# A two-layer expert kernel: the products of layer one and layer two alternate by nine instead of by 27

## The chip, the cores and the metric

The kernel runs on one core of a Trainium2 chip. Its time is the device time in microseconds of one execution. Five engines work side by side and meet only at semaphores: TensorE (PE in the rows, PEld for its weight loads), VectorE (DVE), ScalarE (ACT), GpSimd (POOL) and SyncE (SP), which issues the DMAs.

## The reference

The input x is 32 images of 384 channels and 28 x 28 = 784 pixels. What is computed:

```
xn     = group_norm(x, 32 groups)                         # per image
scores = softmax(xn @ gate_w + gate_b)                    # 4 experts, per pixel
coef   = softmax of the two best scores, given to the experts that were
         picked anywhere as first (weight 0) or second (weight 1)
hdn[e] = relu(w1[e] @ xn + b1[e])                         # 384 -> 384
y[e]   = w2[e] @ hdn[e] + b2[e]                           # 384 -> 384
out    = x + sum over e of coef[e] * y[e]
```

All four experts run on all pixels.

## The kernel before

**Tiles, units, chunks.** The 32 x 784 pixels are cut into 49 tiles of 512 pixels, across image borders. A unit u is one expert of one tile (u = 4t + e, 196 units). A chunk q = 3u + k is one of its three blocks of 128 hidden channels (588 chunks, twelve a tile). Every float32 factor is split into a high and a low part, and a product of two such factors is three matmuls (low x high, high x low, high x high) of 128 x 128 weights with 512 columns. So a chunk of layer one (`mm1`, L432 to L434, into one of the four PSUM banks of `z_ps`) is nine matmuls, and a chunk of layer two (`mm2`, L451 to L453, into the three banks of `y_ps`) is nine as well. `y_ps` adds up over all four experts of a tile.

**One chunk's way.** `mm1` finishes chunk q in `z_ps` and signals `z_ready`. On DVE `scale` (L479) adds the bias and multiplies by the expert's coefficient row, into one of three `hid` buffers; ACT's `split_h_hi` (L486) makes the rounded relu; DVE's `split_h_lo` (L490) the remainder. Then `mm2` of that chunk may run (it waits for `hlo_ready`). In DVE's program, iteration q holds `scale(q + 1)` and then `split_h_lo(q)`, and after these whatever else is due. `mm1` of chunk q waits until `scale` has read chunk q - 4, since there are four banks. After the last `mm2` of a tile (`unit_done`) DVE's `add_product` (L508, three instructions, one for each bank of `y_ps`) adds the product to `res`, which SP then stores; the first `mm2` chunk of the next tile waits, bank by bank, for these three (`out_ready`, L450). `add_product` of tile t - 1 stands in DVE's program at the head of iteration q = 12t + 2.

**What else DVE does.** Every image has to be prepared in good time for its first tile. The pieces hang on chunk numbers (`preparing`): in the tile three before the image's first one, at its chunks 10 and 11, the statistics (L245, and L251 to L262 behind them); in the next tile at chunk 1 the columns of the normalisation (L270 to L273) and half of the normalisation (L278), at chunk 2 the other half, at chunks 8 to 11 the gate (L317 to L358), the last of which makes `wrow`. For images 2 to 31 the first half of the normalisation is thus the last thing ahead of `add_product`. SP writes `wrow` to DRAM (`rows_out`, L524), and reads it back spread over the partitions, for a whole tile (`rows_in`, L531): these are the coefficient rows that `scale` needs from the tile's first chunk on. Image 1 is prepared by hand in tile 0, at q = 2 to 9.

**TensorE's order.** It is written out by hand. The warm-up, the gate product of image 0, and layer one of units 0, 1 and two thirds of unit 2 come first. Then for each unit u: gate products that are due (`gate_product`, L300, 24 short matmuls into `g_ps`), all of `mm1` of unit u + 1 (27 matmuls), the gate product of image 1 if u is 2, and all of `mm2` of unit u (27 matmuls).

Of the kernel before, what the change touches and what calls it, by code (L numbers as in the profile page):

```python
# [9 lines left out]
NK = HID // P  # L10
# [10 lines left out]
UNITS = TILES * E  # L21
# [25 lines left out]
def parts_to(t):  # L47

    return sum(PIECES[:t + 1])
# [7 lines left out]
def first_tile(n):  # L57
    return n * PIX // T
# [6 lines left out]
def conv_moe(nc, x, gate_w, gate_b, w1, b1, w2, b2, out):  # L65
# [7 lines left out]
    with ctx:  # L73
# [6 lines left out]
        def sem(name):  # L80
            return ctx.enter_context(nc.semaphore(name))
# [105 lines left out]
        unit_done = sem("unit_done")  # L187
# [108 lines left out]
        def gate_product(pe, s, n, q):  # L296
            pe.wait_ge(s.xn_ready, HALVES * (n + 1))
            for j in range(NJ):
                for g in range(4):
                    ins = nc.tensor.matmul(g_ps[32 * g:32 * (g + 1), 0:QUART], gw_pad[:, j],  # L300
                                           x_raw[:, q, j, g * QUART:(g + 1) * QUART],
                                           start=(j == 0), stop=(j == NJ - 1), tile_position=(0, 32 * g))
            ins.then_inc(s.gate_ready, 1)
# [70 lines left out]
        def sum_counts(pe, s):  # L374
            pe.wait_ge(s.cnt_ready, 1)
            nc.tensor.matmul(g_ps[:, 0:2 * E], ones[:, :], cnt[:, :, :].rearrange("p r e -> p (r e)"),
                             start=True, stop=True).then_inc(s.cnt_summed, 1)
# [12 lines left out]
        def mm1_early(pe, u, chunks, terms, counts=False):  # L390


            for i, term in enumerate(terms):
                if term == "hl":
                    pe.wait_ge(main.xlo_ready, 1)
                if term == "lh":
                    pe.wait_ge(w1lo_ready, u + 1)
                if term == "hh":
                    pe.wait_ge(main.xhi_ready, 1)
                    pe.wait_ge(whi_ready[0], u + 1)  # L400
                for k in chunks:
                    q = NK * u + k
                    if i == 0 and q >= ZB:
                        pe.wait_ge(early_done, q - ZB + 1)
                    ks = slice(k * P, (k + 1) * P)
                    for j in range(NJ):
                        w = (w1_hi, w1_lo)[term[0] == "l"][:, u, j, ks]
                        x = (x_hi, x_lo)[term[1] == "l"][:, 0, j]
                        ins = nc.tensor.matmul(z_ps[:, q % ZB], w, x, start=(i == 0 and j == 0),
                                               stop=(i == 2 and j == NJ - 1))  # L410
                    if counts and i == 0 and k == 0:
                        sum_counts(pe, main)
                    if i == 2:
                        ins.then_inc(z_ready, 1)

        def mm1(pe, u, chunks=range(NK)):
            t, e = divmod(u, E)
            if t == 0:
                pe.wait_ge(w1lo_ready, 1 + e)
            if e == 0:  # L420
                pe.wait_ge(main.xlo_ready, parts_to(t))
            for k in chunks:
                q = NK * u + k
                if q < ZB + EARLY:
                    pe.wait_ge(early_done, q - ZB + 1)
                else:
                    pe.wait_ge(scaled, q - ZB + 1)
                z = z_ps[:, q % ZB]
                ks = slice(k * P, (k + 1) * P)
                for j in range(NJ):  # L430
                    hi, lo = x_hi[:, t % 2, j], x_lo[:, t % 2, j]
                    nc.tensor.matmul(z, w1_hi[:, e, j, ks], lo, start=(j == 0), stop=False)  # L432
                    nc.tensor.matmul(z, w1_lo[:, e, j, ks], hi, start=False, stop=False)  # L433
                    ins = nc.tensor.matmul(z, w1_hi[:, e, j, ks], hi, start=False, stop=(j == NJ - 1))  # L434
                ins.then_inc(z_ready, 1)

        def mm2(pe, u):
            t, e = divmod(u, E)
            tail = u == UNITS - 1
            if t == 0:  # L440
                pe.wait_ge(w2lo_ready, 1 + e)
            for k in range(NK):
                slot = (NK * u + k) % RING
                pe.wait_ge(hlo_ready, NK * u + k + 1)
                for m in range(NJ):
                    y = y_ps[:, m]
                    ms = slice(m * P, (m + 1) * P)
                    first, last = e == 0 and k == 0, e == E - 1 and k == NK - 1
                    if first and t:
                        pe.wait_ge(out_ready, t * NJ - NJ + m + 1)  # L450
                    nc.tensor.matmul(y, w2_hi[:, e, k, ms], h_lo[:, slot], start=first, stop=False)  # L451
                    nc.tensor.matmul(y, w2_lo[:, e, k, ms], h_hi[:, slot], start=False, stop=False)  # L452
                    ins = nc.tensor.matmul(y, w2_hi[:, e, k, ms], h_hi[:, slot], start=False, stop=last)  # L453
                    if tail and k == NK - 1:
                        ins.then_inc(tail_product, 1)
            if not tail:
                ins.then_inc(unit_done, 1)

        def relu_early(act, q):
            act.wait_ge(z_ready, q + 1)  # L460
# [363 lines left out]
        @block.tensor  # L824
        def _(pe):
            pe.wait_ge(gw_ready, 1)
            pe.wait_ge(main.var_ready, 1)
            for _ in range(WARM):
                nc.tensor.matmul(g_ps[:, 0:P], ones[:, :], ones[:, :], start=True, stop=True)
            gate_product(pe, main, 0, 0)  # L830
            mm1_early(pe, 0, range(NK), ("hh", "lh", "hl"))
            mm1_early(pe, 1, range(NK), ("hh", "hl", "lh"), counts=True)
            mm1_early(pe, 2, range(2), ("hh", "hl", "lh"))
            pe.wait_ge(flag_ready, 1)
            flag = pe.value_load(missing[0:1, 0:1], min_val=0, max_val=1)
            with pe.If(flag > 0):
                with pe.Fori(1, B) as b:
                    gate_product(pe, scan, b - 1, 2)
                sum_counts(pe, scan)

            for u in range(UNITS):
                for n in range(2, B):
                    if NK * u == TILE_CHUNKS * first_tile(n) - LEAD + 8:
                        gate_product(pe, main, n, n % SLOTS)
                if 0 < u < UNITS - 1:
                    mm1(pe, u + 1, chunks=range(2 if u == 1 else 0, NK))
                if u == 2:
                    gate_product(pe, main, 1, 1)
                mm2(pe, u)


# [24 lines left out]
```

## Time and profile before

| | |
|---|---|
| median of 3 runs | 2469.34 us (2468.12 to 2470.34) |
| the profiled execution | 2469.91 us |
| its span, first to last instruction | 2468.1 us |
| mean granted TensorE clock | 0.999 |
| TensorE busy | 2449.9 us, 99% of the span |
| VectorE busy | 1413.7 us, 57% |
| ScalarE busy | 465.6 us, 19% |
| data moved | 189.58 MB, mean 77 GB/s |

The span leaves out 1.8 us of the profiled execution that lie before the first or after the last instruction. A matmul's row is longer than the distance to the next one, since matmuls overlap; the pace is the distance between starts. Idle time of an engine is listed with what ended it.

### The profile page before, as it was taken

How to read it: one execution, taken by the hardware profiler on the slowest of the kernel's cores; microseconds unless marked ns; L12 is line 12 of the kernel's file. 1: busy time of each engine (PE TensorE's matmuls, PEld its weight loads, DVE VectorE, ACT ScalarE, POOL GpSimd, SP SyncE). 2: the span in 40 equal slices, each digit the busy share in tenths (PEclk: the TensorE clock that was granted, in tenths of full speed). 3: DMA queues.
4: the chain of work that ended last, by engine and by line, in shares of the span. 5: the costliest groups of instructions: out<-in, count | busy, mean ns of one | idle time of the engine just before them, and what ended most of it. 6: DMA issues, size and time to landing. Idle time of an engine off the chain costs nothing.

```text
span 2468.1 us, 27782 instructions
## 1 busy us (share of the span) xinstructions
PE 2449.9 (99%) x11372; PEld 2011.4 (81%) x11372; DVE 1413.7 (57%) x2952; ACT 465.6 (19%) x777; POOL 53.3 (2%) x36
## 2 busy tenths in 40 slices
PE   7999999999999999999999999999999999999999
PEld 6788888888888888888888888888888888888887
DVE  7765556556564556545564565556556564556443
ACT  3121111111111121111111121112111111121111
POOL 0000000000000000000000000000000000000000
PEclk9999999999999999999999999999999999999999
DMA  5223122221222213111321123121221222113110
GB/s 185 90 80 104 49 90 69 94 67 49 90 92 71 67 52 123 58 69 49 113 70 69 67 77 107 49 90 69 94 67 49 90 94 68 67 51 108 54 47 26
DMA packets 127520, 189.58 MB, mean 77 GB/s; under 512 B 16032, under 2 KB 80800, under 8 KB 127392
## 3 DMA queue, kind: packets, MB, share of 16 engines
q1 hardware_dynamic: 127392, 187.80, 22.5%
q8 instruction: 89, 1.46, 0.2%
q14 instruction: 39, 0.32, 0.0%
HBM read 146.03 MB, written 41.75 MB: 76 GB/s over the span
## 4 chain that ended last, share of the span: by engine, by line
PE 98%; DVE 1%; DMA 1%; issue 0%; ACT 0%; POOL 0%; SPq 0%; DVEq 0%; POOLq 0%
PE z_ps L432 16%; PE y_ps L451 16%; PE y_ps L452 16%; PE y_ps L453 16%; PE z_ps L434 16%; PE z_ps L433 16%; PE g_ps L300 1%; DMA rows<-rows_dram 0%; DMA rows_dram<-wrow 0%; DMA x_raw<-in_x 0%; DVE w_lo L386 0%; DVE h_lo L490 0%; DVE x_raw L278 0%; ACT h_hi L486 0%; POOL rstd L267 0%
## 5 line engine op out<-in xcount | busy, mean ns | idle before, releaser
L479 DVE SCALAR_TENSOR_TENSOR hid<-z_ps,b_sb,rows 128x512 f32<-128x512 f32 x584 | 436.7, 748 | 896.2 <-PE z_ps L434 892.9
L451 PE MATMUL y_ps<-h_lo,w_hi 128*128 128x512 f32 x1764 | 687.6, 390 | 4.2 <-DVE h_lo L490 4.2
L452 PE MATMUL y_ps<-h_hi,w_lo 128*128 128x512 f32 x1764 | 687.0, 389 | 0.0
L453 PE MATMUL y_ps<-h_hi,w_hi 128*128 128x512 f32 x1764 | 686.9, 389 | 0.0
L432 PE MATMUL z_ps<-x_lo,w_hi 128*128 128x512 f32 x1740 | 680.8, 391 | 0.0
L434 PE MATMUL z_ps<-x_hi,w_hi 128*128 128x512 f32 x1740 | 677.5, 389 | 0.0
L433 PE MATMUL z_ps<-x_hi,w_lo 128*128 128x512 f32 x1740 | 677.0, 389 | 0.0
L486 ACT ACTIVATE h_hi<-hid 128x512 fp32r<-128x512 f32 x588 | 368.6, 631 | 1554.4 <-DVE hid L479 1549.2
L490 DVE SCALAR_TENSOR_TENSOR h_lo<-hid,h_hi 128x512 fp32r<-128x512 f32 x588 | 401.0, 682 | 5.1 <-ACT h_hi L486 4.5
L451 PEld LDWEIGHTS y_ps<-h_lo,w_hi 128*128 128x128 f32 x1764 | 331.6, 188 | 74.4 <-issue 3.1
L432 PEld LDWEIGHTS z_ps<-x_lo,w_hi 128*128 128x128 f32 x1740 | 326.6, 188 | 76.0 <-issue 9.3
L453 PEld LDWEIGHTS y_ps<-h_hi,w_hi 128*128 128x128 f32 x1764 | 331.6, 188 | 68.9
L452 PEld LDWEIGHTS y_ps<-h_hi,w_lo 128*128 128x128 f32 x1764 | 331.6, 188 | 68.5
L434 PEld LDWEIGHTS z_ps<-x_hi,w_hi 128*128 128x128 f32 x1740 | 326.7, 188 | 68.5
L433 PEld LDWEIGHTS z_ps<-x_hi,w_lo 128*128 128x128 f32 x1740 | 326.8, 188 | 67.0
L508 DVE SCALAR_TENSOR_TENSOR res<-y_ps,bias,res 128x512 f32<-128x512 f32 x147 | 101.1, 743 | 111.5 <-PE y_ps L453 111.5
L497 DVE SCALAR_TENSOR_TENSOR res<-rows,bias_gap,res 128x512 f32<-128x512 f32 x147 | 101.5, 746 | 0.0
L267 POOL TENSOR_TENSOR rstd<-gvar_eps,minus_half 128x8 f32<-128x8 f32 x32 | 53.1, 1659 | 2216.7 <-DVE gvar_eps L262 2216.7
L245 DVE BATCH_NORM_STATS2 st<-x_raw 128x6 f32<-128x392 f32 x186 | 92.3, 552 | 0.0
L292 DVE TENSOR_TENSOR x_lo<-x_raw,x_hi 128x1536 fp32r<-128x1536 f32 (+31 forms) x80 | 90.3, 1129 | 0.0
L286 ACT CAST x_hi<-x_raw 128x1536 fp32r<-128x1536 f32 (+31 forms) x80 | 77.1, 964 | 8.8 <-DVE x_raw L278 8.8
L278 DVE TENSOR_SCALAR x_raw<-x_raw,norm 128x1176 f32<-128x1176 f32 (+1 forms) x64 | 69.8, 1093 | 1.2
(88 smaller groups left out, 374.3 us busy)
## 6 DMA issues: line engine op xcount, KB each, us to landing
rows<-rows_dram SPq DMA_DIRECT2D x48, 1280.0 KB, 6.1
x_raw<-in_x SPq DMA_DIRECT2D x62, 588.0 KB, 6.0
res<-in_x SPq DMA_DIRECT2D x18, 768.0 KB, 5.5
out<-res SPq DMA_DIRECT2D x17, 768.0 KB, 4.3
rows_dram<-wrow SPq DMA_DIRECT2D x32, 98.0 KB
w_in<-in_w SPq DMA_DIRECT2D x3, 576.0 KB, 9.9
res<-in_x SPq DMA_DIRECT2D x2, 744.0 KB, 4.9
out<-res SPq DMA_DIRECT2D x2, 744.0 KB, 4.1
```

The lines of the kernel that those rows point to most:

```text
L245: ins = nc.vector.bn_stats(st6[:, HALVES * j + h], x_raw[:, q, j, half(h)])
L432: nc.tensor.matmul(z, w1_hi[:, e, j, ks], lo, start=(j == 0), stop=False)
L433: nc.tensor.matmul(z, w1_lo[:, e, j, ks], hi, start=False, stop=False)
L434: ins = nc.tensor.matmul(z, w1_hi[:, e, j, ks], hi, start=False, stop=(j == NJ - 1))
L451: nc.tensor.matmul(y, w2_hi[:, e, k, ms], h_lo[:, slot], start=first, stop=False)
L452: nc.tensor.matmul(y, w2_lo[:, e, k, ms], h_hi[:, slot], start=False, stop=False)
L453: ins = nc.tensor.matmul(y, w2_hi[:, e, k, ms], h_hi[:, slot], start=False, stop=last)
L479: nc.vector.scalar_tensor_tensor(hid[:, q % HIDS], z_ps[:, q % ZB], b1_sb[:, e, k:k + 1], coef, ALU.add, ALU.mult).then_inc(scaled, 1)
L486: nc.scalar.activation(h_hi[:, q % RING], hid[:, q % HIDS], ACT.Relu).then_inc(hhi_ready, 1)
L490: nc.vector.scalar_tensor_tensor(h_lo[:, q % RING], hid[:, q % HIDS], 0.0, h_hi[:, q % RING].bitcast(f32), ALU.max, ALU.subtract).then_inc ...
L497: lk.inc(nc.vector.scalar_tensor_tensor(xs, rows[:, t % 2, E], bias_gap[:, m:m + 1], xs, ALU.mult, ALU.add))
L508: nc.vector.scalar_tensor_tensor(xs, y_ps[:, m], bias01[:, 1, m:m + 1], xs, ALU.add, ALU.add).then_inc(out_ready, 1)
```

## The change

`mm2` takes the chunks that it is to do, as `mm1` did already, and TensorE's loop goes through the three chunks of a unit, `mm1` of one chunk of unit u + 1 and then `mm2` of the same chunk number of unit u. The matmuls are the same ones. The gate product of image 1, in unit 2, now comes ahead of `mm1` of unit 3, since it stands before the loop over chunks. `unit_done` is still signalled by the unit's last matmul. The other engines' programs are as before.

```
-        def mm2(pe, u):
+        def mm2(pe, u, chunks):
...
-            for k in range(NK):
+            for k in chunks:
...
-            if not tail:
-                ins.then_inc(unit_done, 1)
+                if k == NK - 1 and not tail:
+                    ins.then_inc(unit_done, 1)
...
-                if 0 < u < UNITS - 1:
-                    mm1(pe, u + 1, chunks=range(2 if u == 1 else 0, NK))
                 if u == 2:
                     gate_product(pe, main, 1, 1)
-                mm2(pe, u)
+                for c in range(NK):
+                    if 1 < u < UNITS - 1 or (u == 1 and c == 2):
+                        mm1(pe, u + 1, chunks=[c])
+                    mm2(pe, u, [c])
```

## Rows read from the trace of the kernel before

**Rows 1.** The page: busy time by engine.

```profile
PE 2449.9 (99%) x11372; PEld 2011.4 (81%) x11372; DVE 1413.7 (57%) x2952; ACT 465.6 (19%) x777; POOL 53.3 (2%) x36
```

**Rows 2.** TensorE's waits: us in total, times, longest.

```profile
PE g_ps L829 <- DVE gw_pad L576: 10.4, 1, 10.4
PE y_ps L451 <- DVE h_lo L490: 4.2, 2, 2.1
```

**Rows 3.** Windows: length, PE, PEld, DVE, ACT, POOL busy, clock, DMA, GB/s.

```profile
35.00:38.30 3.30, 3.30 (x8) 2.65 (x9) 3.30 (x7) 1.26 (x2) 0.00 (x0) 0.51 1.04 376
...
77.00:85.00 8.00, 8.00 (x35) 6.61 (x36) 7.61 (x22) 2.53 (x3) 1.64 (x1) 1.00 0.14 51
...
1000.00:2440.00 1440.00, 1440.00 (x6677) 1183.12 (x6677) 807.69 (x1649) 266.29 (x448) 27.83 (x17) 1.00 0.21 72
```

**Rows 4.** Timeline of TensorE: start, length, instruction.

```profile
64.51 0.39 PE L432 MATMUL z_ps<-x_lo,w_hi 128*128 128x512 f32 x1
...
70.40 0.39 PE L434 MATMUL z_ps<-x_hi,w_hi 128*128 128x512 f32 x1
70.63 0.39 PE L451 MATMUL y_ps<-h_lo,w_hi 128*128 128x512 f32 x1
```

**Rows 5.** Timeline of all engines, towards the end.

```profile
2450.06 0.39 PE L434 MATMUL z_ps<-x_hi,w_hi 128*128 128x512 f32 x1
...
2450.55 0.75 DVE L479 SCALAR_TENSOR_TENSOR hid<-z_ps,b_sb,rows 128x512 f32<-128x512 f32 x1 [0.69 <-PE z_ps L434]
...
2452.59 0.75 DVE L479 SCALAR_TENSOR_TENSOR hid<-z_ps,b_sb,rows 128x512 f32<-128x512 f32 x1 [0.69 <-PE z_ps L434]
...
2453.26 1.47 DVE L490 SCALAR_TENSOR_TENSOR h_lo<-hid,h_hi 128x512 fp32r<-128x512 f32 x2
```

**Rows 6.** Timeline of DVE, from chunk 11 of tile 1.

```profile
119.84 0.75 DVE L479 SCALAR_TENSOR_TENSOR hid<-z_ps,b_sb,rows 128x512 f32<-128x512 f32 x1 [4.15 <-PE z_ps L434]
...
127.43 0.74 DVE L479 SCALAR_TENSOR_TENSOR hid<-z_ps,b_sb,rows 128x512 f32<-128x512 f32 x1
...
130.27 2.05 DVE L508 SCALAR_TENSOR_TENSOR res<-y_ps,bias,res 128x512 f32<-128x512 f32 x3
```

**Rows 7.** Timeline of all engines, first matmul of tile 1's layer two.

```profile
84.54 2.05 DVE L508 SCALAR_TENSOR_TENSOR res<-y_ps,bias,res 128x512 f32<-128x512 f32 x3
...
85.08 0.39 PE L434 MATMUL z_ps<-x_hi,w_hi 128*128 128x512 f32 x1
85.39 0.19 PEld L451 LDWEIGHTS y_ps<-h_lo,w_hi 128*128 128x128 f32 x1 [0.34 <-issue]
...
85.98 0.19 PEld L451 LDWEIGHTS y_ps<-h_lo,w_hi 128*128 128x128 f32 x1
```

**Rows 8.** Timeline of DVE, 50 to 76 us.

```profile
50.07 2.09 DVE L278 TENSOR_SCALAR x_raw<-x_raw,norm 128x1176 f32<-128x1176 f32 x2
...
53.55 0.68 DVE L490 SCALAR_TENSOR_TENSOR h_lo<-hid,h_hi 128x512 fp32r<-128x512 f32 x1
58.73 0.41 DVE L317 STREAM_TRANSPOSE lg_pix<-lg_rows 128x224 f32<-128x224 f32 x1 [4.50 <-ACT lg_rows L307]
...
59.72 0.74 DVE L479 SCALAR_TENSOR_TENSOR hid<-z_ps,b_sb,rows 128x512 f32<-128x512 f32 x1
...
62.83 0.75 DVE L479 SCALAR_TENSOR_TENSOR hid<-z_ps,b_sb,rows 128x512 f32<-128x512 f32 x1
...
75.57 0.75 DVE L479 SCALAR_TENSOR_TENSOR hid<-z_ps,b_sb,rows 128x512 f32<-128x512 f32 x1 [3.26 <-DMA rows<-rows_dram]
```

**Rows 9.** Timeline of TensorE in units 2 and 3.

```profile
50.90 0.39 PE L432 MATMUL z_ps<-x_lo,w_hi 128*128 128x512 f32 x1
...
57.11 1.20 PE L300 MATMUL g_ps<-x_raw,gw_pad 128*32 128x196 f32 x24
58.24 0.50 PE L451 MATMUL y_ps<-h_lo,w_hi 128*128 128x512 f32 x1
58.58 0.39 PE L452 MATMUL y_ps<-h_hi,w_lo 128*128 128x512 f32 x1
```

## The prediction, made before the change was run

> **What bounds the kernel now.** I read the page first: TensorE is busy for 2449.9 of 2468.1 us, no other engine for more than 57% [rows 1]. Then the waits of TensorE: 10.4 us before its first matmul and 4.2 us, twice 2.1, for `h_lo` in the first 77 us; beyond these no wait of more than a few tenths is listed [rows 2]. The windows say the same of the long middle: 1440.00 of 1440.00 us busy, at full clock [rows 3]. So the time is the number of matmuls times their pace, plus a start. For the pace I went to TensorE's timeline: 26 distances lie between 64.51 and 70.40, so one is 0.2265 us, and the change from `mm1` to `mm2` at 70.63 is one more such step, 0.23 [rows 4]. Nine matmuls are 2.04 us, eighteen 4.08.
>
> The change removes no matmul and adds none. It can only act by (a) the pace, (b) waits in the steady tiles, (c) the start, (d) the end.
>
> **(a) The pace.** More changes between the layers, six a unit for two, cost nothing where such a change is one plain step [rows 4]. `mm1` in pieces repeats its wait for `x_lo`: two more waits in each of 48 tiles. These have long been met. The waits for `scaled` and `hlo_ready` stood ahead of every chunk before too, with no gap at them. I take nothing. If each of the 96 cost 0.03 us it would be 2.9 us; I have no row for it, and the plain steps across chunks that have such a wait speak for zero.
>
> **(b) The steady tiles.** Three things may come late. I count from S, the start of the matmul that follows layer one's last matmul of chunk 12t + 2. A product's last matmul starts 0.23 before S, and DVE's `scale` starts 0.49 after that start (2450.06, 2450.55 [rows 5]), at S + 0.26.
>
> `h_lo`. `split_h_lo(q)` follows `scale(q + 1)` on DVE, so it needs layer one of chunk q + 1. In the new order 36 matmuls, 8.2 us, lie between that and `mm2` of chunk q (before: 36 for the third chunk of a unit, 63 for the others). DVE needs 0.49 and some 1.4 of this. Its longest iteration, chunk 11 of a tile in which one image ends its gate and another its statistics, with the short iteration after it, takes 119.84 to 127.43, 7.59 us [rows 6]; two chunks give it 8.16. So DVE falls behind by 3.5 us at most and has caught up before chunk 2. The cover holds, with 8.2 - 1.9 - 3.5 = 2.8 us left. Freeing of `z_ps`: 63 matmuls, 54 at least before; more cover. ACT may wait for a gate product ahead of one `split_h_hi`, but its `split_h_lo` waits on DVE for a product which TensorE makes after that gate product, so nothing is later. SP's per-tile loads and stores stand in the same order, at the same pace, with a tile's time (49 us) of cover.
>
> `y_ps`, the tight one. After a tile's last `mm2` there were 27 matmuls of `mm1`, 6.1 us, in which `add_product` could empty `y_ps`; now there are nine, 2.04 us. In 18 tiles DVE only waits for `unit_done`: the add starts at S + 2.04 + 0.26 = S + 2.30. For the images 2 to 31 the columns and half the normalisation stand ahead of it: from the `scale` of chunk 2 to `add_product` 127.43 to 130.27, 2.84 us [rows 6], so it starts at S + 3.10. The first of three adds takes 0.74, and the weight load that waited for it came 0.11 later (84.54 + 0.74 = 85.28, load 85.39 [rows 7]): S + 3.95. It is due one step ahead of the matmul at S + 4.08, at S + 3.85. So it is 0.10 late in 30 tiles, and 0.70 early in the others. What does a late load cost? In tile 1 it was due at 85.08 and came at 85.39, 0.31 late; the next bank's first load came at 85.98 in place of 85.08 + 3 x 0.2265 = 85.76: 0.22 was lost [rows 7]. So some 0.09 are free, and 0.10 late costs about 0.01. The second and third bank follow at 0.66 us on DVE against 0.68 on TensorE, not later. For errors of a few hundredths in each row I take 0.03 a tile, over 29 tiles (tile 1 is counted below): +0.9 us. Bounds: nothing, and 0.25 each (0.34 late) = 7.3 us.
>
> **(c) The start.** Here a chain over DVE and two DMAs decides: gate product of image 1, DVE's gate, `wrow` to DRAM and back, `scale(12)` at 75.57 after a wait for these rows [rows 8], then DVE without a break to `add_product` at 84.54, for which TensorE was 0.22 late at `mm2` of unit 4 [rows 7]. Moved ahead, the gate product waits for image 1's normalisation, which ends at 50.07 + 2.09 = 52.16 [rows 8]. TensorE is there at 50.90 plus the 0.3 that such a product's first load takes [rows 9], so it stands for 1.0 us. The product then runs at 52.2 for 57.11; DVE takes it up when it is free, at 54.15 for 58.73. But `scale(9)` now needs a later product: 52.2 + 1.13 + 0.34 + 7 x 0.2265 + 0.49 = 55.8, for 59.72; and `scale(10)` one 4.08 later, 59.9 for 62.83 [rows 8, 9]. The chain is thus some 3.1 us earlier, not 4.6: rows at 72.4, `split_h_lo(11)` done by 73.8. `mm2` of chunk 11 is due at about 75.8, so the 2.1 us wait goes. `add_product` starts at 81.4. TensorE is at that place at 79.8 already and waits until 82.3, a new wait of 2.4 us. From there to the end of unit 4 it has 45 matmuls left (`mm2` 12, `mm1` 16, `mm2` 13, `mm1` 17, `mm2` 14) where it had 27. So: -3.1 + 18 x 0.2265 = **+1.0 us**. Bounds: if the chain comes no earlier, +4.1; if it is early enough not to be waited for, 1.0 - 2.3 - 0.2 = -1.5.
>
> **(d) The end.** Layer one's last chunk ends nine matmuls before unit 194 does; `scale` to the end of the last `h_lo` takes 2452.59 to 2454.73, 2.1 us [rows 5], and that `h_lo` is due 27 matmuls, 6.1 us, after layer one's end. Nothing.
>
> **Sum.** +1.0 + 0.9 = +1.9 us. The profiled execution took 2469.91, its span 2468.1 and 1.8 around it; it lies 0.6 over the median of 2469.34, within the runs' spread. I add to the median: **2471.2 us**. A measurement of this kernel can tell about 0.2%, 4.9 us, from no change.
>
> **Rivals.** (1) The emptying of `y_ps` is the new bound: slower. All hangs on 0.10 us worked out of 3.95. If the add comes 0.22 later still, since `z_ready` or `unit_done` take longer or DVE is held by something, each of 29 tiles costs 0.22: 6.4 + 1.0, 2476.7. It decides from (4.9 - 1.0) / 29 = 0.13 us a tile. Against it: the rows used are of the same instructions in the same order. (2) The chain at the start is earlier than I have it, and the new wait doesn't arise: 2469.34 - 1.5 = 2467.8, still no change. (3) The new wait of 2.4 us lowers the clock. Of the two waits of 2.1 us [rows 2], the first, up to 35 us, was followed by a granted clock of 0.51 until 38.3, the 1.2 GHz level; after the second, up to 77 us, it stayed 1.00, 2.4 GHz [rows 3]. Eight matmuls took 3.30 us there, 0.41 each for 0.2265: a drop would cost about 1.5 us: 2472.7. (4) The pace itself depends on the order of products, and 0.2265 is not what a matmul must take: at 512 columns and 2.4 GHz the columns alone are 0.2133. If alternating took off half of the 0.013 over it, 10,500 matmuls would give 69 us, 2400. Against it: `z_ps`, nine in a row into one bank, and `y_ps`, three, run at one pace [rows 4]. The Trainium skill (TensorE: Matmul & The Clock Gate, on 56 ns against 53.3) has 215.7 ns for back-to-back matmuls of 512 columns at full clock. The rows here show 226.5 in both layers, so the measurement decides; by the page's pace, reached through the new order, the time would be near 2355 us, an estimate.
>
> **How the numbers follow.** Forecast, near +1.9: 0.62. Rival 1: 0.18, slower by over 0.2%. Rival 2: 0.12 and rival 3: 0.05, both within 0.2%. Rival 4: 0.03, faster. So faster 0.03, within 0.2% 0.79, slower 0.18. The range goes from rival 2, less 0.6 for the spread, 2467.2, to the start's +1.0 with the upper bound of (b), 7.3, a little under 2477.7: 2477.5.
>
> **What would show it.** Right: TensorE 99% busy, the pace still 0.2265; one wait of about 1 us before L300 near 51 us; none before the L451 of chunk 11; one of some 2.4 us before the L451 near 80 us, ended by L508; in 30 tiles the first L451 load at most 0.1 late and `add_product` without idle time ahead of it there. Wrong: L451 waiting for L508 by 0.2 us or more at 30 places (rival 1), waits of L451 for L490 in steady tiles (the cover miscounted), waits of L432 for L479, another distance between matmuls (rival 4), or a granted clock under 1 after 82 us (rival 3).

## The result, and the profile after

The changed kernel takes 2474.70 us (median of 11 runs, 2471.49 to 2476.44), the kernel before 2469.91 in the same comparison (11 runs, 2468.12 to 2471.12). The ratio is 1.0018, with a 95% interval of 1.0011 to 1.0026: some 4.5 us more (4.8 between the two medians). The loss is clear of the noise, and a little under the 0.2% that were taken as the bound of no change. 2471.2 was forecast, 1.9 us more, with a range of 2467.2 to 2477.5. The profiled execution took 2475.36 us, its span 2473.6.

The page of the changed kernel, busy time by engine (answers to [rows 1]):

```profile
PE 2453.0 (99%) x11372; PEld 2010.1 (81%) x11372; DVE 1425.5 (58%) x2952; ACT 471.2 (19%) x777; POOL 53.3 (2%) x36
```

TensorE is as full as before, with the same 11372 matmuls. Its waits in the changed kernel (answers to [rows 2]: us in total, times, longest):

```profile
PE g_ps L829 <- DVE gw_pad L576: 10.4, 1, 10.4
...
PE g_ps L300 <- DVE x_raw L278: 2.7, 1, 2.7
PE y_ps L451 <- DVE res L508: 2.1, 1, 2.1
PE y_ps L451 <- DVE h_lo L490: 1.8, 1, 1.8
```

The second wait for `h_lo` is gone, and the two that were forecast stand there: for image 1's normalisation ahead of its gate product, and for `add_product`. None is listed in a steady tile. So where did the time go? I split the run by two rows that both orders have, the last matmul of tile 1 and that of tile 46. Timeline of TensorE, kernel before:

```profile
129.51 0.39 PE L453 MATMUL y_ps<-h_hi,w_hi 128*128 128x512 f32 x1
...
2372.54 0.39 PE L453 MATMUL y_ps<-h_hi,w_hi 128*128 128x512 f32 x1
```

and changed kernel:

```profile
133.64 0.39 PE L453 MATMUL y_ps<-h_hi,w_hi 128*128 128x512 f32 x1
...
2378.00 0.39 PE L453 MATMUL y_ps<-h_hi,w_hi 128*128 128x512 f32 x1
```

Tiles 2 to 46 took 2243.03 us before and 2244.36 after: +1.3. Tile 1's end comes 4.1 later. The first matmul of layer two, kernel before and changed kernel:

```profile
34.95 0.77 PE L451 MATMUL y_ps<-h_lo,w_hi 128*128 128x512 f32 x1 [2.10 <-DVE h_lo L490]
```

```profile
34.96 0.47 PE L451 MATMUL y_ps<-h_lo,w_hi 128*128 128x512 f32 x1 [1.79 <-DVE h_lo L490]
```

So the start, from there to tile 1's end, went from 94.56 to 98.68. The end adds nothing: the spans differ by 2473.6 - 2468.1 = 5.5 = 4.1 + 1.3, within the rounding.

The start of the changed kernel, timeline of two engines (answers to [rows 8, 9] and the first row of [rows 7]):

```profile
52.22 1.26 PE L300 MATMUL g_ps<-x_raw,gw_pad 128*32 128x196 f32 x24 [2.71 <-DVE x_raw L278]
53.41 0.80 PE L432 MATMUL z_ps<-x_lo,w_hi 128*128 128x512 f32 x1
54.01 0.63 PE L433 MATMUL z_ps<-x_hi,w_lo 128*128 128x512 f32 x1
54.43 0.63 PE L434 MATMUL z_ps<-x_hi,w_hi 128*128 128x512 f32 x1
...
57.35 0.75 DVE L479 SCALAR_TENSOR_TENSOR hid<-z_ps,b_sb,rows 128x512 f32<-128x512 f32 x1 [2.14 <-PE z_ps L434]
...
74.00 0.75 DVE L479 SCALAR_TENSOR_TENSOR hid<-z_ps,b_sb,rows 128x512 f32<-128x512 f32 x1 [3.31 <-DMA rows<-rows_dram]
...
82.96 2.05 DVE L508 SCALAR_TENSOR_TENSOR res<-y_ps,bias,res 128x512 f32<-128x512 f32 x3
83.84 0.66 PE L451 MATMUL y_ps<-h_lo,w_hi 128*128 128x512 f32 x1 [2.12 <-DVE res L508]
84.30 0.63 PE L452 MATMUL y_ps<-h_hi,w_lo 128*128 128x512 f32 x1
84.73 0.63 PE L453 MATMUL y_ps<-h_hi,w_hi 128*128 128x512 f32 x1
```

The reader is to see two things. The gate product begins at 52.22, as forecast; but the matmuls behind it start 0.42 apart (54.01, 54.43), not 0.23, and so `scale(9)` comes at 57.35 where 55.8 was worked out, the rows at 74.00 for 72.4, `add_product` at 82.96 for 81.4. And behind the second wait the matmuls are slow once more. The windows of the changed kernel say why (answers to [rows 3]: length, PE, PEld, DVE, ACT, POOL busy, clock, DMA, GB/s):

```profile
35.00:38.30 3.30, 3.30 (x15) 2.73 (x16) 3.30 (x7) 1.27 (x2) 0.00 (x0) 1.00 1.04 375
53.40:57.00 3.60, 3.60 (x13) 2.87 (x10) 1.71 (x6) 1.07 (x3) 0.00 (x0) 0.55 0.00 0
57.00:81.70 24.70, 24.70 (x110) 20.11 (x108) 19.01 (x60) 4.70 (x8) 1.64 (x1) 1.00 0.35 111
83.80:87.70 3.90, 3.86 (x10) 3.10 (x11) 3.90 (x6) 0.63 (x1) 0.00 (x0) 0.56 0.35 132
88.00:2440.00 2352.00, 2352.00 (x10910) 1928.27 (x10909) 1341.29 (x2732) 439.51 (x732) 47.47 (x29) 1.00 0.22 74
```

Behind each of the two new waits the granted clock was at the 1.2 GHz level for some eight matmuls, 8 x 0.2 = 1.6 us each (0.43 apart in place of 0.23). In this execution it was not lowered at 35, where it was in the execution before.

A steady tile with an image's normalisation, the begin of tile 4 (timeline of the changed kernel):

```profile
234.27 2.05 DVE L508 SCALAR_TENSOR_TENSOR res<-y_ps,bias,res 128x512 f32<-128x512 f32 x3
235.12 0.19 PEld L451 LDWEIGHTS y_ps<-h_lo,w_hi 128*128 128x128 f32 x1 [0.16 <-issue]
235.23 0.39 PE L451 MATMUL y_ps<-h_lo,w_hi 128*128 128x512 f32 x1
...
235.72 0.19 PEld L451 LDWEIGHTS y_ps<-h_lo,w_hi 128*128 128x128 f32 x1
```

The load came 0.74 + 0.11 after the add's start. Loads stand 0.04 apart in the plain stream (0.2265 - 0.188), here 0.16: it was 0.12 late; 0.10 was forecast. Between the ends of tiles this costs 0.02 to 0.07 in each of the 29 tiles with an image (tiles 2 to 46), and 0.00 in the others.

### The profile page after: what moved, and what is told of

Read it like the earlier page. It is cut to its first block, busy times and chain, and to the rows that moved or that the text cites. A ratio compares the mean times of both kernels' runs of the same rounds, so it can differ in the third digit from the quotient of the medians.

```text
span 2473.6 us, 27888 instructions
## 1 busy us (share of the span) xinstructions
PE 2453.0 (99%) x11372; PEld 2010.1 (81%) x11372; DVE 1425.5 (58%) x2952; ACT 471.2 (19%) x777; POOL 53.3 (2%) x36
## 4 chain that ended last, share of the span: by engine, by line
PE 97%; DVE 2%; DMA 1%; issue 0%; POOL 0%; SPq 0%; ACT 0%; DVEq 0%; POOLq 0%
PE z_ps L432 16%; PE y_ps L451 16%; PE y_ps L452 16%; PE y_ps L453 16%; PE z_ps L434 16%; PE z_ps L433 16%; PE g_ps L300 1%; DMA rows<-rows_dram 0%; DVE h_lo L490 0%; DMA rows_dram<-wrow 0%; DMA x_raw<-in_x 0%; DVE w_lo L386 0%; DVE x_raw L278 0%; DVE hid L479 0%; POOL rstd L267 0%
## 5 line engine op out<-in xcount | busy, mean ns | idle before, releaser
L451 PE MATMUL y_ps<-h_lo,w_hi 128*128 128x512 f32 x1764 | 687.6, 390 | 3.9 <-DVE res L508 2.1
L453 PE MATMUL y_ps<-h_hi,w_hi 128*128 128x512 f32 x1764 | 687.2, 390 | 0.0
L451 PEld LDWEIGHTS y_ps<-h_lo,w_hi 128*128 128x128 f32 x1764 | 331.4, 188 | 77.7 <-issue 9.3
L453 PEld LDWEIGHTS y_ps<-h_hi,w_hi 128*128 128x128 f32 x1764 | 331.6, 188 | 69.7
L508 DVE SCALAR_TENSOR_TENSOR res<-y_ps,bias,res 128x512 f32<-128x512 f32 x147 | 100.9, 742 | 17.1 <-PE y_ps L453 17.1
```

Source lines behind the costliest of these rows:

```text
L508: nc.vector.scalar_tensor_tensor(xs, y_ps[:, m], bias01[:, 1, m:m + 1], xs, ALU.add, ALU.add).then_inc(out_ready, 1)
```

## The experiments

My theory: the order itself costs nothing. The time is a start cost, made of new waits in units 2 to 4 and of the lowered clock behind them, and 0.03 to 0.07 us in each tile where DVE comes late to empty `y_ps`. The main rival: alternating costs a little everywhere.

The table has for each kernel the medians beside those of the kernel before on the same chip, and from its one profiled execution the start (first L451 to the last L453 of tile 1), where in it the clock was lowered, and tiles 2 to 46 (from there to the last L453 of tile 46). All are differences of starts in the timeline.

| kernel | median | before | ratio (95%) | start | clock lowered behind | tiles 2 to 46 |
|---|---|---|---|---|---|---|
| before | 2469.91 | | | 94.56 | 35 us | 2243.03 |
| changed | 2474.70 | 2469.91 | 1.0018 (1.0011 to 1.0026) | 98.68 | L300, L508 | 2244.36 |
| 1: alternating from unit 5 | 2470.16 | 2468.41 | 1.0006 (0.9997 to 1.0015) | 93.10 | - | 2244.31 |
| 2: alternating to unit 4 | 2471.97 | 2468.41 | 1.0012 (1.0003 to 1.0021) | 97.15 | 35 us, L508 | 2243.02 |
| 3: changed, later add | 2505.65 | 2468.41 | 1.0150 (1.0135 to 1.0166) | 96.52 | - | 2273.09 |
| 4: before, later add | 2470.01 | 2468.41 | 1.0007 (0.9997 to 1.0016) | 94.05 | - | 2243.02 |
| 5: changed, gate after chunk 9 | 2471.47 | 2468.78 | 1.0009 (1.0000 to 1.0018) | 94.57 | 35 us | 2243.99 |
| 6: before, gate after chunk 9 | 2466.87 | 2468.78 | 0.9989 (0.9980 to 0.9998) | 91.48 | - | 2243.02 |
| 7: 27 at a tile's start | 2467.02 | 2468.78 | 0.9991 (0.9982 to 1.0000) | 91.10 | - | 2243.02 |
| 8: changed, wait filled | 2472.02 | 2468.78 | 1.0012 (1.0003 to 1.0021) | 95.51 | 35 us | 2244.04 |
| 9: as 1, earlier add | 2469.84 | 2469.38 | 1.0001 (0.9991 to 1.0010) | 94.39 | 35 us | 2243.02 |
| 10: before, gate after chunk 10 | 2466.71 | 2468.96 | 0.9993 (0.9984 to 1.0002) | 90.95 | - | 2243.02 |
| 11: changed again | 2474.19 | 2468.96 | 1.0021 (1.0012 to 1.0030) | 97.21 | 35 us, L508 | 2244.39 |
| 12: as 8, again | 2472.86 | 2468.96 | 1.0016 (1.0007 to 1.0025) | 95.55 | - | 2244.41 |

**1 and 2, the change in two parts.** TensorE's loop in 1, and in 2 with the branches exchanged:

```
-                if u == 2:
-                    gate_product(pe, main, 1, 1)
+                if u < 5:
+                    if u > 0:
+                        mm1(pe, u + 1, chunks=range(2 if u == 1 else 0, NK))
+                    if u == 2:
+                        gate_product(pe, main, 1, 1)
+                    mm2(pe, u, range(NK))
+                else:
                     for c in range(NK):
-                        if 1 < u < UNITS - 1 or (u == 1 and c == 2):
+                        if u < UNITS - 1:
                             mm1(pe, u + 1, chunks=[c])
                         mm2(pe, u, [c])
```

> Units 0 to 4 in the old order, alternation from unit 5 on. Theory (the added time is a start cost of some 4 us, from new waits in units 2 to 4 and a lowered clock behind them, plus 0.03 to 0.07 us at each tile where an image's normalisation stands ahead of add_product): 29 such tiles x 0.045 = +1.3 us over the kernel before, no wait of TensorE for L508, no slow matmuls after 40 us. Rival (alternating itself costs, spread over all units): 191 of 196 units alternate, so nearly the whole +4.5 us stays.

> The other half alone: alternation in units 1 to 4, with the gate product of image 1 ahead of layer one of unit 3; the old order from unit 5 on. Theory: +1.0 us if the clock is not lowered in the start, up to +4.1 us if it is lowered after both new waits (before L300 near 50 us and before L451 near 83 us), and nothing added in any later tile. Rival: nearly nothing is added, 4 of 196 units alternate.

1 added 1.28 us in tiles 2 to 46 and nothing in the start (93.10 is less than 94.56 because the clock was not lowered at 35 in its execution); its time alone can't be told from no change, since its interval holds 1. 2 added nothing in the tiles. Waits of TensorE in 2:

```profile
PE g_ps L829 <- DVE gw_pad L576: 9.4, 1, 9.4
PE y_ps L451 <- DVE h_lo L490: 2.3, 1, 2.3
PE y_ps L451 <- DVE res L508: 2.2, 1, 2.2
PE g_ps L300 <- DVE x_raw L278: 1.1, 1, 1.1
```

and its windows behind L300 and behind L508:

```profile
52.60:56.00 3.40, 3.40 (x19) 2.81 (x16) 2.70 (x8) 1.07 (x3) 0.00 (x0) 1.00 0.00 0
81.60:86.00 4.40, 4.40 (x12) 3.46 (x13) 4.40 (x6) 0.63 (x1) 0.00 (x0) 0.61 0.46 159
```

Here the clock was lowered behind one of the two new waits, and the start was 97.15, 1.5 less than in the changed kernel's profile. Four units make most of the added time, 191 the smaller part: the rival is out. The medians say the same, +1.75 and +3.56.

**3 and 4, one DVE instruction moved, in both orders.** The second half of the normalisation goes ahead of `add_product`:

```
                         normalise(dve, main, n, n % SLOTS, 0, HALF)
-                    if off == 4:
                         normalise(dve, main, n, n % SLOTS, HALF, PIX)
```

> The changed kernel with the second half of every image's normalisation (images 2 to 31, one DVE instruction of 1.02 us) moved ahead of add_product. The computation is the same. Theory (the emptying of y_ps has 0.09 us to spare after a late load of 0.10): add_product starts 1.02 later, the first load of layer two is 1.1 late, each of 29 tiles costs some 1.05 us: +30 us over the changed kernel's steady tiles, +34 us over the kernel before, and TensorE waits for L508 at about 30 places. Rival (DVE's order at the tile's head has room): under +6 us.

> The kernel before with the same move of the second half of the normalisation ahead of add_product. Theory: with 27 matmuls between a tile's last product and the next tile's first there are some 4 us to spare, so nothing is added in a steady tile; in tile 1, where DVE is late already, the first product of layer two waits 1.0 us longer: +1.0 us. Rival (the move itself costs, by DVE's order): +30 us as in the changed kernel.

In the changed order tiles 2 to 46 took 30.06 us more than before, 1.04 a tile with an image; in the old order nothing more. Waits of TensorE in 3:

```profile
PE y_ps L451 <- DVE res L508: 25.2, 30, 3.1
```

Thirty waits, one for each image from 2 to 31. The profiled execution of 3, at full clock, lies 34.3 over the median of the kernel before, as worked out; the other three, at a lower mean clock, lie 37 over it. So the new order leaves no room at this place, and 27 matmuls leave more than the 1.0 us that was tried. In 4 that wait is there once, 0.9 us, in tile 1; the start, 94.05, is 0.95 over that of 1, which has the old order and no lowered clock.

**5, 6, 7 and 10, the gate product of image 1.** In 5 it is moved in the changed kernel, in 6 in the old order, in 10 one chunk later; 7 is 6 with the alternating loop in all units from 5 on but the first of each tile:

```
# 6
+                if u == 2:
+                    mm1(pe, 3, chunks=[0])
+                    gate_product(pe, main, 1, 1)
+                    mm1(pe, 3, chunks=[1, 2])
+                elif 0 < u < UNITS - 1:
-                if 0 < u < UNITS - 1:
                     mm1(pe, u + 1, chunks=range(2 if u == 1 else 0, NK))
-                if u == 2:
-                    gate_product(pe, main, 1, 1)
                 mm2(pe, u)
# 5
-                if u == 2:
-                    gate_product(pe, main, 1, 1)
                 for c in range(NK):
                     if 1 < u < UNITS - 1 or (u == 1 and c == 2):
                         mm1(pe, u + 1, chunks=[c])
+                    if u == 2 and c == 0:
+                        gate_product(pe, main, 1, 1)
                     mm2(pe, u, [c])
# 7
+                elif u < 5 or u % E == 0:
+                    (mm1 of unit u + 1, then mm2 of unit u, 27 and 27)
+                else:
+                    (alternating by nine)
# 10
-                    mm1(pe, 3, chunks=[0])
+                    mm1(pe, 3, chunks=[0, 1])
                     gate_product(pe, main, 1, 1)
-                    mm1(pe, 3, chunks=[1, 2])
+                    mm1(pe, 3, chunks=[2])
```

> The changed kernel, but the gate product of image 1 comes after layer one of chunk 9 and not ahead of it. Theory: image 1's normalisation is then done, so the wait before L300 goes, and with it the slow matmuls behind it; scale(9) no longer queues behind the gate product, so DVE's chain to add_product of tile 0 is some 4.1 us earlier than in the kernel before and the 45 matmuls that follow it eat just that. Start 0 (up to +1.5 where the wait for L508 near 80 us lowers the clock), tiles +1.3: +1.3 to +2.8 us over the kernel before. Rival (the place of the gate product doesn't matter): +4.5 us as the changed kernel.

> The kernel before (27 and 27), with the gate product of image 1 after layer one of chunk 9. Theory: the chain is some 4.5 us earlier and nothing waits for it: the 2.1 us wait for h_lo near 75 us and the 0.2 us at tile 1 go. -2.5 us against the kernel before. Rival (the wait near 75 us has another cause): 0.

> Alternation by nine in three of four units from unit 5 on, 27 and 27 in the first unit of each tile and in units 0 to 4, and the gate product as in the run with 27 and 27. Theory (all that alternation costs in a steady tile is the short time to empty y_ps): nothing is added per tile, so the time of the run with 27 and 27 and the moved gate product, -2.5 us. Rival (alternating costs elsewhere too): +1 or more over that run.

> 27 and 27, with the gate product of image 1 one chunk later than in the first such run, after layer one of chunk 10. There TensorE stood 1.0 us before L300. Theory: it comes 2 us later now, so that wait goes, and the chain to add_product, 1 us later, still has 2 us to spare: 1.0 us less than the run with the product after chunk 9, about -3 us against the kernel before, -1.5 where that has a lowered clock in neither. Rival (no room left): the same as that run.

5 came out as expected: no wait before L300, one of 2.4 for L508, a start of 94.57 as in the kernel before (94.56, both with the clock lowered at 35), +0.96 in the tiles. That execution is one of its two fastest; its median is 2.7 over the kernel before. 6 is the first version that beats both kernels, by 0.1%, just outside the noise (0.9980 to 0.9998). Waits of TensorE in 6:

```profile
PE g_ps L829 <- DVE gw_pad L576: 10.9, 1, 10.9
PE y_ps L451 <- DVE h_lo L490: 2.2, 1, 2.2
PE g_ps L300 <- DVE x_raw L278: 1.7, 2, 1.0
```

One wait for `h_lo` is left, at the first matmul of layer two; that near 75 us is gone. Its start is 1.6 under the 93.10 of 1, not 2.5, since 1.0 of a wait before this L300 came instead (the other wait in that row, 0.7, stands at image 0's gate product): in an execution without the lowered clock at 35 TensorE is at that place earlier. 7 has 6's time, and its tiles cost nothing, 2243.02, though three units of four alternate. With 9 below, where all units from 5 on alternate for nothing once the add comes earlier, this shows that emptying `y_ps` is the only thing that alternating costs in a steady tile; and alternating gives nothing for it. In 10 the wait before L300 went, but the start fell by 0.5 only, not by 1.0: the chain had no 2 us to spare, and TensorE's steps at 73.05 and 81.49 are longer by 0.2 and 0.15. 6, 7 and 10 can't be told apart by their times, and the intervals of 7 and 10 reach 1.

**8 and 12, the wait for `add_product` filled.** Nine matmuls of 512 columns into `g_ps`, a product that is not part of the computation and that nobody reads (the wait ahead of them is for `g_ps` to be free):

```
+                    if u == 4 and c == 0:
+                        pe.wait_ge(main.gate_copied, 2)
+                        for _ in range(9):
+                            nc.tensor.matmul(g_ps[:, 0:T], w1_hi[:, 0, 0, 0:P], x_hi[:, 1, 0], start=True, stop=True)
                     mm2(pe, u, [c])
```

> The changed kernel with nine more matmuls of 512 columns into g_ps (a spare product that nobody reads) in unit 4, ahead of the layer two that waits for add_product. Theory: they take 2.04 us and fit into that wait, so they cost nothing by themselves; the wait is filled, the clock is not lowered behind it, and the eight or nine slow matmuls there go: up to 1.5 us less than the changed kernel, in the executions in which the clock was lowered there. Rival (the slow matmuls have nothing to do with the pause): the same time or up to 2.0 us more.

> The changed kernel with nine spare matmuls in the wait for add_product in unit 4, as before, now on the same chip as the changed kernel. Theory: no slow matmuls behind 80 us; 0.8 to 1.6 us less than the changed kernel, since the clock is lowered there in half or more of its executions. Rival: no difference, or longer by the nine matmuls.

> The changed kernel itself, beside the others of this call. Theory: +4.5 us over the kernel before, of which 1.3 in the tiles, 2.5 in the start, and 1.6 for each time that the clock is lowered behind the wait for L300 or for L508; executions 1.6 us apart. Rival (first comparison was chance): within 2 us of the kernel before.

The first matmul of layer two in 8, and the nine in its wait for `add_product`:

```profile
34.27 0.47 PE L451 MATMUL y_ps<-h_lo,w_hi 128*128 128x512 f32 x1 [2.19 <-DVE h_lo L490]
...
79.36 2.20 PE L853 MATMUL g_ps<-x_hi,w_hi 128*128 128x512 f32 x9
80.72 2.05 DVE L508 SCALAR_TENSOR_TENSOR res<-y_ps,bias,res 128x512 f32<-128x512 f32 x3
81.60 0.47 PE L451 MATMUL y_ps<-h_lo,w_hi 128*128 128x512 f32 x1
```

The window behind L508 in 8, and the one of 11, the changed kernel on the same chip as 12:

```profile
81.50:86.00 4.50, 4.46 (x20) 3.68 (x20) 4.50 (x6) 0.63 (x1) 0.00 (x0) 1.00 0.43 150
```

```profile
83.00:87.70 4.70, 4.70 (x15) 3.70 (x14) 4.01 (x5) 0.63 (x1) 0.00 (x0) 0.64 0.73 227
```

In both profiles of the filled kernel the clock was full there and the start 95.5. That the extra matmuls are free is shown: layer two begins 0.88 after the add's start (81.60 - 80.72), as it does unfilled in the changed kernel (83.84 - 82.96). That they keep the clock up is not shown. 12 took 1.3 us less than 11, but the intervals of the two ratios overlap; one of eleven executions, in 8 and in 12, took some 2.5 us more than the mean of the others; and in 5 and 3 the clock stayed up behind waits of 2.4 and 3.1 us that nothing filled.

**9, room made for the add.** Kernel 1 with the first half of the normalisation behind `add_product` too:

```
                     if off == 3:
                         norm_columns(dve, main, n, lk)
-                        normalise(dve, main, n, n % SLOTS, 0, HALF)
                     if off == 4:
+                        normalise(dve, main, n, n % SLOTS, 0, HALF)
                         normalise(dve, main, n, n % SLOTS, HALF, PIX)
```

> Units 0 to 4 in the old order, alternation from unit 5 on, and the first half of every normalisation (images 2 to 31) moved behind add_product, beside the second half. The computation is the same. Theory: the first load of layer two is then 0.9 us early in every tile, so the 0.03 to 0.07 us at 29 tiles go, and with tile 1 the 0.2 us there: the time of the kernel before, less 0.2. Rival: the +1.3 us of the run without this move stay.

Tiles 2 to 46 are back at 2243.02 us, and the start is 0.2 under that of the kernel before (94.39, the clock lowered at 35 in both). The time is the kernel before's, 1.0001.

**The start, added up.** The old order has 93.1 without a lowered clock (1) and 94.4 to 94.6 with one at 35 (before, 9). The changed order has 95.5 without one that matters (8 and 12, the filled kernel; 3, unfilled, has 96.52 with an add that is 1.0 later, which agrees), 97.2 with one behind L508 (2, 11), and 98.7 with one behind L300 as well (changed). A lowered clock at 35 costs it nothing, since TensorE then waits 1.1 in place of 2.7 for image 1 (2 and 11 against the changed kernel and 12). Each lowering that matters is thus worth 1.5 to 1.7 us, and the rest of the start's cost is 95.5 - 93.1 = 2.4, or 1.0 against an execution like the one profiled before. The times agree: beside 11, the executions whose mean granted clock was 1.000 took 2472.17 us in the changed kernel (mean of two) and 2468.35 in the kernel before (mean of 15). That is 3.8 apart, for 2.4 + 1.3 = 3.7, so most of the loss is there without any lowered clock.

## Why the prediction was right, and where it was off

*What bounds the kernel, and (a), the pace.* Right. The pace is 0.23 in both orders, and in 7 three units of four alternate for 0.00 us. The rival with the pace (4) is out: nothing went faster.

*(b), the tight place.* Right in mechanism and place, and close in number. The load for the first `mm2` of a tile was 0.12 late in tile 4, 0.10 was worked out; it cost 0.02 to 0.07 us in each of 29 tiles, 1.34 in all (1.0 to 1.4 in the five kernels that alternate so: 1, 5, 8, 11, 12), for 0.9 forecast; 3 and 9 moved it both ways. The working itself gave 0.01 a tile, and the 0.03 was an allowance for errors of the rows, so that the sum came near is in part the allowance. Tiles without an image lost nothing, and no other cover failed: `h_lo`, `z_ps` and SP wait nowhere. Rival 1, the emptying of `y_ps` as the new bound, was not there (it was to decide from 0.13 us a tile); 3 shows what it would have cost, 30 us at 1.0 us more.

*(c), the start.* Here the sum was mis-sized: +1.0 forecast, +4.1 in the profiled pair. The parts were there, the gate product at 52.2, the `h_lo` wait gone, a new wait of 2 us for `add_product`, 45 matmuls behind it. The chain was worked out rightly as far as it goes: from the first L451 to `add_product` it takes 84.54 - 34.95 = 49.6 us before, and 80.72 - 34.27 = 46.45 in 8, the 3.1 less that were forecast (its row for `scale(10)` gives 2.9 by itself). What failed is the pricing of rival 3, the lowered clock, at a chance of 0.05 and for one drop. Its own rows had shown one lowering behind two waits of 2.1 us, and the sign that it named, a granted clock under 1 after 82 us, is there (0.56). In the profiled execution it came twice: behind L300 it also held up the chain, whose 3.1 us came down to 84.54 - 82.96 = 1.6, and behind L508 it cost another 1.6. Without either, the start is 95.5 by 8, and 95.5 - 94.56 is the +1.0 that was worked out, with the clock lowered at 35 in both. A second thing was not reckoned with: that lowering at 35 stood in the rows, but it belongs to some executions of the kernel before only. In the old order it costs 1.5 us, in the changed order nothing, and the sum was added to a median over both sorts. Of 27 runs of the kernel before, in the comparison with 1 to 4, 16 took 2467.5 to 2468.5 us at a mean granted clock of 1.000 and 11 took 2469.0 to 2470.8 at 0.999. The changed order loses 2.4, not 1.0, in the start against the first sort.

*(d), the end.* Right: after tile 46 the two kernels run alike, 95.6 us to the end of the span (2468.1 - 2372.54 and 2473.6 - 2378.00).

*Rival 2*, a chain so early that nothing waits for it, did not come: L451 waited for L508 in each unfilled start that alternates (changed, 2, 3, 5, 11). Only with 27 and 27 in the first units and the gate product moved is the wait gone: 6, 7 and 10, with -1.9, -1.8 and -2.3 us of median.

*Luck.* That the time lies inside the range is in part luck. The upper end was made of late loads in 29 tiles, 7.3 us, of which 1.3 came; the time came from the start instead, where the prediction had +4.1 as a bound for a chain that comes no earlier at all, not for lowered clocks. And the time stayed within 0.2% by little (1.0018).

The sum is now: 2.4 or 1.0 in the start, 1.3 in the tiles, and 1.6 for each lowered clock, of which the changed kernel has up to two; that is 2.3 to 6.9, and 4.8 was measured (2474.70 - 2469.91), 5.2 in run 11. The profiled pair has 1.0 + 1.3 + 2 x 1.6 = 5.5, which is the difference of its spans.

## What to carry to other kernels

Where one engine is 99% busy with the same instructions in both orders, reordering can only move waits: list, for each wait, how many instructions of the bound engine lie between the signal and the need, before and after. Interleaving evens out most of these distances but shortened the one at the tile's end from 27 to 9, and whether that hurts hung on one DVE instruction of 1.0 us (nothing, 1.3 us or 30 us). And price a pause of TensorE at the pause plus the slow matmuls that may follow (here 1.6 us); look in the start of the profile whether it happened there, and read several executions before a sum is made against one.

## What the runs showed of the hardware that was not expected

Whether a pause lowers TensorE's clock is not told by its length in these runs. It was lowered behind waits of 2.1, 2.2, 2.2 and 2.7 us (changed, 2, 11, changed), and not behind waits of 2.4, 2.7, 2.7 and 3.1 us (5, 3, 12, 3). Nor is it told by the kernel: the changed kernel has it at 35 us in 11 and not in its first profile. In the kernel before, the executions with a mean granted clock of 0.999 took 1.4 to 1.9 us more on average than those with 1.000, in each of the four sets of its runs that stand beside 1 to 12. What decides it is open.
